# Decoder layer with routed experts on one core: pairs of GpSimd scatters that wait for their landing, and slot weights placed behind the copy of the next tile's rows

## What is computed

```python
x = _layernorm(x + attn(x)); x = _layernorm(x + xattn(x, ctx))
gate_probs = softmax(x @ gate_w + gate_b)
weights, selected = top_k(gate_probs, 2); weights = weights / sum(weights)
comb = zeros((n, E)).at[arange(n)[:, None], selected].set(weights)
h = gelu(einsum('nd,edf->enf', x, w1) + b1[:, None, :])
expert_out = einsum('enf,efd->end', h, w2) + b2[:, None, :]
x = _layernorm(x + einsum('ne,end->nd', comb, expert_out))
```

## Time and profile before

| | us |
|---|---|
| median of 3 runs (lowest, highest) | 583.77 (583.11, 585.3) |
| the profiled execution: its time | 584.04 |
| the profiled execution: its span | 582.0 |
| self-attention, to about | 276 |
| cross-attention and routing, to the first hidden product of tile 0 | 433 |
| 19 expert tiles, to the last output product | 564 |
| sum of the two result rows, layer norm, output | 582 |

### The profile page before, as it was taken

How to read it: one execution, slowest core, us unless ns; L and a number is a source line. 1 busy time by engine, 2 the same in 40 slices (tenths; PEclk the granted TensorE clock), 3 DMA queues, 4 the chain that set the end, 5 groups by cost and what they waited for, 6 DMA issues and landing times. The chain is left out here.

```text
span 582.0 us, 12798 instructions
## 1 busy us (share of the span) xinstructions
PE 544.0 (93%) x3908; PEld 470.7 (81%) x3908; DVE 363.5 (62%) x1192; ACT 315.8 (54%) x864; POOL 166.5 (29%) x269
## 2 busy tenths in 40 slices
PE   6999999999999999999998999999589999999970
PEld 4889899898998989899897566655368999999960
DVE  3465655656556465655667766787466576666775
ACT  4664554645545455464556878777343455555524
POOL 3511312113121221300346658541513111112122
PEclk9999999999999999999999999999799999999995
DMA  8630300303002030081000000010212454552434
GB/s 257 238 116 18 128 20 18 109 18 127 18 23 104 18 127 0 31 341 79 2 2 0 2 2 4 2 75 10 74 47 74 179 183 159 203 188 66 165 100 145
DMA packets 19973, 50.49 MB, mean 87 GB/s; under 512 B 3072, under 2 KB 9472, under 8 KB 17504
## 3 DMA queue, kind: packets, MB, share of 16 engines
q1 hardware_dynamic: 15536, 31.01, 15.6%
q10 hardware_dynamic: 2448, 13.37, 6.1%
q0 software_dynamic: 1952, 5.65, 2.7%
HBM read 35.85 MB, written 14.11 MB: 86 GB/s over the span
## 5 line engine op out<-in xcount | busy, mean ns | idle before, releaser
L1384 ACT ACTIVATE hT<-bank,b 128x128 f32<-128x128 f32 x152 | 53.2, 367 | 60.8 <-PE bank L992 57.3
L992 PE MATMUL bank<-xgT,w 128*128 128x128 f32 x608 | 71.6, 276 | 0.8 <-DVE xgT L1707 0.8
L992 PEld LDWEIGHTS bank<-xgT,w 128*128 128x128 f32 x608 | 69.6, 192 | 1.3 <-issue 1.3
L1127 ACT ACTIVATE Pr<-Sm,nmax 128x128 f32<-128x128 f32 x64 | 25.8, 403 | 70.6 <-DVE nmax L1453 70.5
L1453 DVE CUSTOM_DVE_ANT_0 Sm<-bank,mask 128x128 f32<-128x128 f32 (+1 forms) x128 | 40.7, 356 | 29.2 <-PE bank L697 29.2
L633 PE MATMUL bank<-xT_hi,wqk_hi 128*128 128x512 f32 x124 | 54.1, 437 | 0.2 <-ACT QT L1111 0.2
L1593 DVE TENSOR_REDUCE xnmax<-bank 128x2 f32<-128x512 f32 x64 | 43.5, 688 | 16.1 <-PE bank L856 15.5
L567 POOL DMA_INDIRECT y_rows<-ys,row_i x19 | 19.8, 1044 | 103.0 <-DVE ys L1738 103.0
L635 PE MATMUL bank<-xT_hi,wqk_lo 128*128 128x512 f32 x124 | 49.0, 395 | 0.0
L634 PE MATMUL bank<-xT_lo,wqk_hi 128*128 128x512 f32 x124 | 48.7, 392 | 0.0
L1475 DVE TENSOR_TENSOR z_lo<-bank,z_hi 128x256 fp32r<-128x256 f32 x64 | 27.1, 424 | 30.8 <-ACT z_hi L1120 30.6
(11 more groups left out here) (259 smaller groups left out, 1493.4 us busy)
## 6 DMA issues: line engine op xcount, KB each, us to landing
w<-in_w ACTq DMA_DIRECT2D x12, 1024.0 KB, 6.3
x_slots<-w SPq DMA_DIRECT2D x16, 516.0 KB, 5.0
w_raw<-in_w_attn SPq DMA_DIRECT2D x31, 256.0 KB, 3.5
w<-in_w SPq DMA_DIRECT2D x4, 1024.0 KB, 7.9
xg<-x_slots SPq DMA_DIRECT2D x18, 129.0 KB
acc<-in_x SPq DMA_DIRECT2D x1, 1024.0 KB, 9.3
ctxT<-in_ctxT SPq DMA_DIRECT2D x1, 1024.0 KB, 7.4
w_x<-in_w_x SPq DMA_DIRECT2D x1, 1024.0 KB, 8.4
```

The lines of the kernel that those rows point to most:

```text
L992: last = mm(ps_h[f % 4][:, 0:P], w1[e % 2][:, c, f * P:(f + 1) * P], xgT[:, c, :], start=c == 0, stop=c == DC - 1)
L1384: A(hT[:, f, :], ps_h[f % 4][:, 0:P], ACT.Gelu_apprx_tanh, bias=b1[:, e, f:f + 1])\
```

## The change

GpSimd's `scatter(0)` gets a wait and an empty instruction in front of the scatters of tiles 1, 2 and 3: each waits until all scatters issued so far, 2, 4 and 6 of them, have landed. The condition `t % 1 == 0` always holds. Rounds 1 and 2 are as they were, but stand behind round 0 on the same engine. On DVE `slot_weights()` moves from the front of tile 1's closing work to its end.

```diff
                 for t in range(t0, t1):
+                    if r == 0 and 0 < t and t % 1 == 0:
+                        pool.wait_ge(s["xs_written"], 16 * 2 * t)
+                        pool.nop(nofuse=True)
                     for k in range(2):
                         g.indirect_dma_start(xs_d, bass.IndirectOffsetOnAxis(ap=slot_i[:, t, k:k + 1], axis=0),
                                              acc_rows[:, t, :], None).then_inc(s["xs_written"], 16)
...
                 else:
-                    slot_weights()
                     rows_of(e, xg_s[:, e, D:W])
                     xgt_evac(e + 3)
                     y_add(e, e)
+                    slot_weights()
```

## The result

| | before | after |
|---|---|---|
| median of 6 runs (lowest, highest) | 583.94 (583.11, 585.3) | 587.33 (585.96, 588.24) |
| ratio of the runs, 95% interval | | 1.0053 [1.0032, 1.0074] |
| the profiled execution: time, span | 584.04, 582.0 | 585.96, 583.9 |

The forecast was 583.9 in a range of 581.0 to 586.3. The profiled execution after is the lowest of its six, so its trace accounts for 1.9 of the 3.4 us between the medians. Taken by itself it lies inside the predicted range; the median, 1.0 us above the range, does not.

The account below looks back on a forecast made before the run. PE, busy for 93% of the span, was taken to bound the kernel, with a 5.0 us wait for ACT's zt. Profiled 584.04 - 2.1 (stall) - 0.2 (weights) + 2.4 (clock) = 584.1; median 583.9 us, range 581.0 to 586.3.

Parts of the forecast that it names:

- The stall goes: At ACT's copy of zt in round 0: the waits remove 5.0 us, the copy starting at 411.65 and not 416.61.
- ACT waits for code: At ACT's zt: code delivery is held up while scatters follow without a pause, causing the 5.0 us of standing still.
- the packet of the earlier trace: One packet of an instruction queue at 409.0, amid round 0's scatters, taken as the only sign of code fetching.
- a pause let it through: Round 0: the first pair lands by 409.1, the next starts at 409.6, and code gets through in between.
- the second rival: ACT's stall has nothing to do with the scatters; late scatters stay hidden, only the moved weights gain: 583.6 us, chance 0.16.
- The price of a wait: GpSimd's three waits in round 0: 3.0 us each, between 2.86 and 3.19, making the eighth scatter 5.0 us later.
- the promised gain of 2.1 us: Tile 0's first hidden product starts at 430.9, 2.1 us earlier, limited by the late loads of xg_s.
- The clock: PE idles 3.4 us before the xg_s transposes and its clock falls, costing 2.4 us, between 0 and 3.5.
- The weights: DVE's slot weights, moved behind tile 1's result, shrink PE's idle 0.84 us ahead of tile 2's hidden products by 0.2 us.
- The sum: Whole kernel: 584.04 - 2.1 - 0.2 + 2.4 = 584.1 for the profiled execution, 583.9 us for the median.
- The forecast's own mechanism: Round 0 onward: stall gone, xg_s loads late, PE's clock lost for a while; chance 0.45, own range 582.0 to 586.0.
- the third rival: ACT's stall lasts as long as round 0, so the three waits stretch it by 5.0 us: 588.6 us, chance 0.12.

Follow-up runs that it names:

- The fillers: Changed kernel with 24 unused filler matmuls on PE between the gate's product and the transposes waiting for xg_s; 585.29 us, ratio 1.0096 to before.
- The change again: The changed kernel itself, unaltered, run once more in the second session beside the kernel before; 587.38 us, ratio 1.0059.
- the twelve: Changed kernel with only its first wait, plus twelve filler matmuls on PE ahead of the xg_s transposes; 580.78 us, ratio 1.0015 in the third session.

## Why the prediction was wrong

**The stall goes: right, for a reason that was not.** Zt was due at 411.7 and came at 412.19; PE's gate was due to end at 426.0 and ended at 426.07. That ACT waits for code is refuted: moved code changed nothing, DVE is held as well, and the packet of the earlier trace rows is there without a stall. Nor did a pause let it through: in the trace of after it lies at 408.75 to 409.00, and the first pair landed at 409.33. The Trainium skill's page Runtime: NRT & Kernel Launch, section Instruction fetch mechanics, which holds that fetches are mostly hidden, agrees with that. But the second rival, which I had hung on it, fell too: the stall does depend on the scatters. That the stall was there to be removed was luck, too: in four of the five later sessions it was not.

**The price of a wait: this is the step that failed.** I gave each 3.0 us, between 2.86 and 3.19, and got 3.71, 3.43 and 4.06, outside both bounds. The lower one took SyncE's 2.56 us from scatter to issue, and a new scatter's 0.30, as if GpSimd woke up like that. The upper one, was measured on a result scatter late in the kernel. Measured here, a wait is a landing of 2.67 to 3.29 us, 0.27 for the wake-up and 0.46 for the empty instruction, an operation to which I had given no price of its own. The eighth scatter was due at 419.3 and came at 421.59, 2.2 of the 2.3 us through the three waits; everything behind carries this on, as the sum had it: SyncE 429.28 for 426.9, the transposes 431.90 for 429.4. Of the promised gain of 2.1 us at the first hidden product a loss was left.

**The clock: right in kind, too high in size.** I put 2.4 us, between 0 and 3.5, with the clock back after 5 us of work. It was back 3.5 us after PE's restart, in the slice 435 to 436. The fillers put the price at 1.5 us. In the trace of after it is 434.38 - 431.90 - 1.49 = 1.0 us ahead of the hidden products and 0.5 in them. Since 1.0 of it lies ahead of the first hidden product, that one is late by 2.5 from the waits and the loads and by 1.0 from the clock: 430.9 was said, 434.38 came.

**The weights: nothing against it.** 0.2 us was said, and the measured ratio, 1.0001 [0.9982, 1.002], cannot tell that from nothing. The timeline of DVE and PE of after shows the order that the prediction described:

```profile
448.53 0.17 DVE L1709 COPY token<-xg 128x2 f32<-128x2 f32 x1 [1.28 <-PE bank L984]
...
449.17 3.83 PE L995 MATMUL bank<-xgT,w 128*128 128x128 f32 x32 [0.67 <-DVE xgT L1710]
449.34 0.22 DVE L1758 TENSOR_TENSOR slot_t<-slot,slot_lh 128x64 f32<-128x64 f32 x1
...
450.62 0.22 DVE L1760 TENSOR_REDUCE w_lh<-slot_t 128x8 f32<-128x64 f32 x1
...
452.29 0.36 DVE L1729 CAST hT_hi<-hT 128x384 fp32r<-128x384 f32 x1 [1.45 <-ACT hT L1387]
```

PE's gap is 0.67 and not 0.84, and the weights end at 450.84, long before DVE is due again.

**The sum.** In the profiled executions: 1.34 us at the first hidden product and 0.56 behind it (583.9 - 434.38 against 582.0 - 433.04), together the 1.9 us between the spans. In the terms of the prediction: instead of a gain of 2.1 us a loss of 0.3 to 0.4, since the transposes came 2.5 late; 1.5 for the clock and not 2.4; nothing to see for the weights. The error of the clock, 0.9, hid part of that of the waits. The median lies 1.4 higher. The change again, profiled at 587.43, has that too: its landings took 3.37, 2.96 and 2.96 us, its first hidden product started at 434.99 and the hidden products of tile 0 took 4.95 us. So it is more of the same two things, landing and clock.

**The chances.** No rival came true. The forecast's own mechanism ended beyond its range: I had named a wake-up of 3.5 us with a full loss of clock as one way to lose more than 2.9 us, and gave it and the third rival 0.15 together, while my bounds for the wake-up stopped at 3.19. The range was too narrow on the strength of two rows, neither of which was this wait.

## What to carry to other kernels

A wait that breaks a queue of transfers into pieces costs, per wait, the whole landing of the last transfer and the wake-up of the waiting engine, and it is paid by everything that is queued behind it; add up the instructions in the wait, the empty ones too, and take the landing from the same kind of transfer at the same place. Before removing a stall whose releaser the profile cannot name, find out whether it is there on another day. And where a new wait opens a gap in PE's work, filler matmuls in it give the clock back, and cost nothing as long as they end before what PE waits for has come; here the twelve ended 0.1 us ahead of the transposes.

## What was not expected of the hardware

- A stall that comes and goes: the same kernel took 584.15 us in one session and 579.87 in another on the same chip. While it lasts, what PE has finished reaches ACT and DVE up to 6 us late beside a stream of GpSimd's scatters. In the same session one more such stream delayed it by no more than 0.7 us.
- An empty instruction behind a wait on GpSimd costs 0.46 us (0.73 us from landing to the next scatter with it, 0.27 without).
- Scatters of the same size landed 2.45 to 3.64 us after their start, and some occupied GpSimd for 1.3 to 1.6 us where most took 0.96.
- The clock lost in a gap of PE cost 1.5 us by the rows, behind a gap of 6.4 us as behind one of 3.5.
